# Perceiver layer on one core: the opening's loads, transposes and scalars issued in another order

## The reference

```python
x = x + cross(layernorm(x), ctx)   # K_hat = cos((ctx Wk + bk) Wr + br); softmax((xn Wq + bq) K_hat^T) (ctx Wv + bv)
x = x + attn(layernorm(x))         # the 8 most similar earlier tokens of h, softmax over them, message from h
    # mix = sigmoid(log_mix); scale = softplus(log_scale) + 0.01
    # gelu((mix h + (1 - mix) message) * gain + bias) * scale
x = x + moe(layernorm(x))          # 8 experts, one per token by argmax: gelu(x W1 + b1) W2 + b2, times the top probability
```

## Time and profile before

| | us |
|---|---|
| median of 3 runs | 442.94 |
| lowest, highest | 440.27, 447.44 |
| profiled execution, whole | 446.33 |
| its span, first to last instruction | 444.2 |
| TensorE busy in the span | 411.5 (93%) |
| VectorE, ScalarE, GpSimd busy | 248.5, 255.9, 237.7 |

### The profile page before, as it was taken

How to read it: one execution, slowest core, us unless ns; L and a number is a source line. 1 busy time by engine, 2 the same in 40 slices (tenths; PEclk the granted TensorE clock), 3 DMA queues, 4 the chain that set the end, 5 groups by cost and what they waited for, 6 DMA issues and landing times.

```text
span 444.2 us, 10438 instructions
## 1 busy us (share of the span) xinstructions
PE 411.5 (93%) x3121; PEld 281.9 (63%) x3121; DVE 248.5 (56%) x808; ACT 255.9 (58%) x582; POOL 237.7 (54%) x458
## 2 busy tenths in 40 slices
PE   7977999999999999999898878889999999999991
PEld 7423445454455544545344667679999999998991
DVE  2637478878988888788788655543222222222210
ACT  1474777888888988888678745253333232424240
POOL 1760567767788788888667765451222232222210
PEclk9987999999999999999999998999999999999997
DMA  9897899896986987789999624765685656465100
GB/s 174 188 251 214 216 273 273 202 214 174 278 186 150 240 202 212 185 206 260 190 296 310 220 79 132 234 173 206 239 304 187 200 180 217 165 192 198 57 0 2
DMA packets 119450, 87.46 MB, mean 197 GB/s; under 512 B 78622, under 2 KB 109088, under 8 KB 119268
## 3 DMA queue, kind: packets, MB, share of 16 engines
q1 hardware_dynamic: 111460, 75.96, 62.7%
q0 software_dynamic: 3744, 9.46, 7.0%
q10 hardware_dynamic: 4192, 1.38, 1.7%
HBM read 79.15 MB, written 8.53 MB: 197 GB/s over the span
## 4 chain that ended last, share of the span: by engine, by line
PE 71%; SPq 15%; issue 4%; DMA 4%; DVE 2%; ACT 1%; another core or an unknown queue 1%; POOL 0%; DVEq 0%; ACTq 0%; POOLq 0%
PE pK L1513 19%; PE pT L1500 17%; SPq L575 10%; PE pK L1475 8%; PE pT L1475 7%; PE b L1420 3%; SPq L570 3%; PE b L1659 3%; PE b L1554 3%; PE b L1619 2%; PE b L1598 2%; DMA f_row<-rows_by_token,token_i 2%; DMA token_i<-tokens_by_expert 2%; SPq L563 1%; PE b L1648 1%
## 5 line engine op out<-in xcount | busy, mean ns | idle before, releaser
L1272 ACT ACTIVATE XF<-pT,b_now 128x128 f32<-128x128 f32 x184 | 52.7, 370 | 97.1 <-PE pT L1500 91.8
L1513 PE MATMUL pK<-W,XF 128*128 x368 | 86.6, 387 | 5.9 <-issue 4.1
L1500 PE MATMUL pT<-XF,stage 128*128 128x128 f32 x736 | 87.0, 275 | 0.3 <-issue 0.3
L1500 PEld LDWEIGHTS pT<-XF,stage 128*128 128x128 f32 x736 | 85.9, 192 | 2.1 <-issue 1.1
L1513 PEld LDWEIGHTS pK<-W,XF 128*128 128x128 f32 x368 | 68.8, 193 | 15.5 <-issue 6.9
L409 POOL DMA_INDIRECT f_row<-rows_by_token,token_i x23 | 23.8, 1035 | 83.3 <-DMA out_dram<-XF,token_i 70.3
L1475 PE MATMUL pK<-stage,Wkr 128*128 128x512 f32 x128 | 63.0, 618 | 0.0
L1475 PE MATMUL pT<-stage,Wkr 128*128 128x512 f32 x128 | 61.8, 606 | 1.1 <-DVE stage L726 1.1
L1247 ACT ACTIVATE stage<-stage 128x512 f32<-128x512 f32 x64 | 40.7, 637 | 12.8 <-DVE stage L787 12.6
L787 DVE TENSOR_TENSOR stage<-stage 128x512 f32<-128x512 f32 x64 | 46.2, 722 | 0.7
L726 DVE STREAM_TRANSPOSE stage<-XF 128x1024 f32<-128x1024 f32 x32 | 39.5, 1234 | 12.4 <-DMA XF<-in_ctx_dram 11.3
(11 more groups left out here) (196 smaller groups left out, 666.1 us busy)
## 6 DMA issues: line engine op xcount, KB each, us to landing
stage<-in_L_ffn_W_dram SPq DMA_DIRECT2D x23, 1024.0 KB, 5.4
stage<-in_ctx_dram SPq DMA_DIRECT2D x32, 512.0 KB, 5.4
XF<-in_ctx_dram SPq DMA_DIRECT2D x248, 64.0 KB
W<-in_L_ffn_W_dram SPq DMA_DIRECT2D x8, 1024.0 KB
rows_by_token<-rows_out SPq DMA_DIRECT2D x16, 256.5 KB
ctx_last<-in_ctx_dram SPq DMA_DIRECT2D x64, 32.0 KB, 4.5
X<-in_x_dram SPq DMA_DIRECT2D x1, 1536.0 KB, 7.8
tokens_by_expert<-no_token POOLq DMA_DIRECT2D x2, 576.0 KB, 4.2
```

The lines of the kernel that those rows point to most:

```text
L1272: ins = act.activation(f_hT[b][:, n * P:(n + 1) * P], pT[i][:, (n % 4) * P:(n % 4 + 1) * P], ACT.Gelu, bias=b1_now[:, b, n:n + 1])
L1500: mm = pe.matmul(pT[i][:, (n % 4) * P:(n % 4 + 1) * P], W1[q][:, c, n * P:(n + 1) * P], f_inT[:, q % 2, c * P:(c + 1) * P], start=c == 0, ...
L1513: mm = pe.matmul(p_out, f_hT[q % 2][:, n * P:(n + 1) * P], W2[:, bass.ds(e, 1), n, :].rearrange("p o d -> p (o d)"), start=n == 0, stop=n ...
```

## The change

SyncE issues (1, 0)'s first part only; ScalarE issues its second. The rows of group 0 come next, then (1, 1), then (2, 0), and only then bv, Wv, the rows of group 1 and the small weights. GpSimd loads the two logs at the start. ScalarE issues Wq, bq, Wqk first, computes the scalars ahead of its half of `Wkr`, issues the second part of (1, 0), and loads the Sin table after that; `turn(0, 1)`, `turn(0, 3)` and `sine(0, 0, 2)` move forward by a place each, and in step 1 the Exp table is loaded right behind `turn(1, 0)`. VectorE turns (0, 1) before its first `whole` and (1, 0) after the third unit, and does its scalars in the prologue. TensorE's `ctx_project(1, 0, 1)` stands behind scores(0) and xn_T(1), as in later steps. The mask of own tokens is built with the other masks. At g = 15 `load_tokens(0)` stands ahead of `next_group(15)`.

```diff
--- before.py
+++ after.py
@@ -326,6 +326,8 @@
             keep(ident[:], [[-1, P]], 0, 1, ALU.not_equal, 1.0)
             made_at["ident"] = n[0]
             made(pool.memset(minus_half[:], -0.5))
+            for k, name in enumerate(("log_mix", "log_scale")):
+                pool.dma_start(logs[:, k:k + 1], a["L0_attn_" + name].partition_broadcast(P)).then_inc(S["logs_ld"], 16)
             rstd_x(0)
             normal_x(0)
@@ -363,13 +365,13 @@
                     for j in range(BG):
                         keep(t[j * T:(j + 1) * T, :], [[-1, T]], 0, 1, ALU.is_gt, fill)
                 made(pool.memset(unpicked[:], UNPICKED))
-                made_at["masks"] = n[0]
-
-            def own_parts():
-
                 made(pool.memset(own_part[:], 0.0))
                 for j in range(BG):
                     keep(own_part[j * T:(j + 1) * T, :], [[-1, T]], 0, 1, ALU.not_equal, 1.0)
+                made_at["masks"] = n[0]
+
+            def own_parts():
+
                 pool.wait_ge(S["scal_dve"], 3)
                 made(pool.tensor_scalar(own_part[:], own_part[:], sc[:, 2:3], None, ALU.mult))
@@ -582,20 +584,19 @@
                 sp.dma_start(last_rows[:, k * P:(k + 1) * P].rearrange("b (a n) -> b a n", n=T),
                              in_blocks(c_in[:, CF, :], k)).then_inc(S["last_ld"], 16)
             sp.wait_ge(S["ctxT_r"], 1)
-            for j in range(2):
-                load_by_feature(1, 0, j)
+            load_by_feature(1, 0, 0)
+            load_ctx(0, 0)
+            load_last(0, 0)
             sp.wait_ge(S["ctxT_r"], 2)
             for j in range(2):
                 load_by_feature(1, 1, j)
-            load_ctx(0, 0)
-            load_last(0, 0)
+            sp.wait_ge(S["ctxT_r"], 3)
+            for j in range(2):
+                load_by_feature(2, 0, j)
             sp.dma_start(bv[:], a["L0_xattn_bv"].partition_broadcast(P)).then_inc(S["bv_ld"], 16)
             sp.dma_start(Wv[:], rows(a["L0_xattn_Wv"])).then_inc(S["w_ld"], 16)
             load_ctx(1, 1)
             load_last(1, 1)
-            sp.wait_ge(S["ctxT_r"], 3)
-            for j in range(2):
-                load_by_feature(2, 0, j)
             sp.dma_start(gain[:], a["L0_attn_gain"].partition_broadcast(P)).then_inc(S["w_ld"], 16)
             sp.dma_start(gbias[:], a["L0_attn_bias"].partition_broadcast(P)).then_inc(S["w_ld"], 16)
             sp.dma_start(Wroute[:], rows(a["L0_ffn_Wr"])).then_inc(S["w_ld"], 16)
@@ -653,6 +654,8 @@
                     sp.wait_ge(S["ctxT_r"], 2 * g + 1)
                     for j in range(2):
                         load_by_feature(g + 1, 0, j)
+                if g == NG - 1:
+                    load_tokens(0)
                 next_group(g, g % 2)
                 if g == 2:
                     sp.wait_ge(S["consts"], made_at["routing"])
@@ -660,8 +663,6 @@
                         sp.dma_start(by_token[TOK + i:TOK + i + 1, :], rows_out[0:1, 0, :]).then_inc(rows_st[i], 16)
                 if g >= 3 and g % 2:
                     load_w2(g // 2 - 1)
-                if g == NG - 1:
-                    load_tokens(0)
                 if g % 2 and g >= 7:
                     keep((g - 7) // 2)
                 if g == NG - 2:
@@ -1025,17 +1026,18 @@
                 v.wait_ge(S["xn_r"], g)
                 moments(g, st1, mv1, "st1_r", "mv1_r")
+            ctx_turned(0, 1)
             whole(0, 0)
             fraction(0, 0)
-            ctx_turned(0, 1)
             next_stats(1)
             whole(0, 1)
             fraction(0, 1)
             next_moments(1)
             last_copy()
-            ctx_turned(1, 0)
+            scalars()
             whole(0, 2)
             fraction(0, 2)
+            ctx_turned(1, 0)
             last_turned()
             whole(0, 3)
             fraction(0, 3)
@@ -1100,8 +1102,6 @@
                 residual(s - 1)
                 if s >= 4:
                     logits_copy(s - 4)
-                if s == 1:
-                    scalars()
                 if s == 13:
                     plan_experts(0)
                 if s == 14:
@@ -1215,22 +1215,23 @@
             for q in range(P // T):
                 act.dma_start(*quarter_by_feature(0, 1, 1, q)).then_inc(by_feature_ld[1], 16)
             act.wait_ge(S["consts"], made_at["ident"])
-            act.activation(sumA[:], ident[:, 0:1], ACT.Sin)
+            act.dma_start(Wq[:], rows(a["L0_xattn_Wq"])).then_inc(S["wq_ld"], 16)
+            act.dma_start(bq[:], col(a["L0_xattn_bq"]), allow_slow_non_contiguous=True).then_inc(S["wq_ld"], 16)
+            act.dma_start(Wqk[0:H, :], a["L0_attn_W_q"]).then_inc(S["wqk_ld"], 16)
+            act.dma_start(Wqk[H:2 * H, :], a["L0_attn_W_k"]).then_inc(S["wqk_ld"], 16)
+            act.wait_ge(S["logs_ld"], 2 * 16)
+            act.activation(sc[:, 0:1], logs[:, 0:1], ACT.Exp, scale=-1.0).then_inc(S["scal_act"], 1)
+            act.activation(sc[:, 5:6], logs[:, 1:2], ACT.Abs).then_inc(S["scal_act"], 1)
+            act.wait_ge(S["scal_act"], 2)
+            act.activation(sc[:, 6:7], sc[:, 5:6], ACT.Exp, scale=-1.0).then_inc(S["scal_act"], 1)
+            act.wait_ge(S["scal_act"], 3)
+            act.activation(sc[:, 7:8], sc[:, 6:7], ACT.Ln, bias=1.0).then_inc(S["scal_act"], 1)
             act.wait_ge(S["wkr_mm"], 2)
             act.mul(Wkr[:, 1, :], pT[1][:, 0:D], INV_2PI).then_inc(S["wkr_half"], 1)
-            act.dma_start(bq[:], col(a["L0_xattn_bq"]), allow_slow_non_contiguous=True).then_inc(S["wq_ld"], 16)
-            act.dma_start(Wq[:], rows(a["L0_xattn_Wq"])).then_inc(S["wq_ld"], 16)
-            act.dma_start(Wqk[0:H, :], a["L0_attn_W_q"]).then_inc(S["wqk_ld"], 16)
-            act.dma_start(Wqk[H:2 * H, :], a["L0_attn_W_k"]).then_inc(S["wqk_ld"], 16)
-
-            def scalars():
-                act.wait_ge(S["logs_ld"], 2 * 16)
-                act.activation(sc[:, 0:1], logs[:, 0:1], ACT.Exp, scale=-1.0).then_inc(S["scal_act"], 1)
-                act.activation(sc[:, 5:6], logs[:, 1:2], ACT.Abs).then_inc(S["scal_act"], 1)
-                act.wait_ge(S["scal_act"], 2)
-                act.activation(sc[:, 6:7], sc[:, 5:6], ACT.Exp, scale=-1.0).then_inc(S["scal_act"], 1)
-                act.wait_ge(S["scal_act"], 3)
-                act.activation(sc[:, 7:8], sc[:, 6:7], ACT.Ln, bias=1.0).then_inc(S["scal_act"], 1)
+            act.wait_ge(S["ctxT_r"], 1)
+            for q in range(P // T):
+                act.dma_start(*quarter_by_feature(1, 0, 1, q)).then_inc(by_feature_ld[0], 16)
+            load_table(ACT.Sin, 0)
             def turn(g, u):
@@ -1317,31 +1318,29 @@
             act.wait_ge(S["bkr_cp"], 1)
             turn(0, 0)
+            turn(0, 1)
             act.dma_start(X[:, 2:4, :], x_v[:, 2:4, :]).then_inc(S["xnext_ld"], 16)
-            turn(0, 1)
             xnT_copy(0)
             sine(0, 0, 0)
-            act.dma_start(logs[:, 0:1], a["L0_attn_log_mix"].partition_broadcast(P)).then_inc(S["logs_ld"], 16)
-            act.dma_start(logs[:, 1:2], a["L0_attn_log_scale"].partition_broadcast(P)).then_inc(S["logs_ld"], 16)
             sine(0, 0, 1)
             turn(0, 2)
+            turn(0, 3)
             queries(0)
+            sine(0, 0, 2)
             act.wait_ge(S["last_fr"], 4)
             act.activation(khat_last[:], last_frac, ACT.Sin, scale=TWO_PI).then_inc(S["khat_last_r"], 1)
-            turn(0, 3)
-            sine(0, 0, 2)
             sine(0, 0, 3)
             for s in range(1, NG):
                 if s >= 3:
                     second_exp(s - 3)
                 turn(s, 0)
+                if s == 1:
+                    load_table(ACT.Exp, 1)
                 xnT_copy(s)
                 first_exp(s - 1)
                 if s >= 7 and s % 2:
                     router_exp(s // 2 - 3)
-                if s == 1:
-                    scalars()
                 if s >= 4:
                     gelu_y(s - 4)
                 probsT_copy(s - 1)
@@ -1680,15 +1679,12 @@
             for s in range(1, NG):
                 ctx_project(s, 0, 0)
-                if s == 1:
-                    ctx_project(s, 0, 1)
                 scores(s - 1)
                 if s >= 7 and s % 2:
                     pe.wait_ge(S["logits_r"], s - 4)
                     rank(s // 2 - 3)
                 xn_T(s)
-                if s >= 2:
-                    ctx_project(s, 0, 1)
+                ctx_project(s, 0, 1)
                 probs_T(s - 1)
                 if s >= 2:
                     h_T(s - 2)
```

## The result

The changed kernel takes 446.31 us (median of 20 runs, 443.77 to 450.07), the kernel before 443.10 beside it (20 runs). The ratio is 1.0087, 95% interval [1.0058, 1.0117]: slower by 3.9 us or 0.9%, clear of noise but within the 2% that the chances were given for. The forecast was 436.4 and its range 432.0 to 441.0; the result lies above the range, and its sign is the other one.

A forecast was written before the change was run, and what follows sets the result against it. TensorE was taken as the bound (71% of the span), with 9.8 us to draw on in two early steps. Terms -5.5 - 2.1 + 0.6 + 0.5 = -6.5 us gave 436.4 against the 442.94 median; eight in ten between 432.0 and 441.0.

The forecast's parts named there:

- the mechanism of step 1 up to (2, 0): Step 1: SyncE issues (2, 0) earlier, so it is turned at 30.1 instead of 35.5, 5.4 us earlier.
- step 1 at -5.5: Step 1's gain: step 2 starts at 36.1, not 41.62; -5.5 us, bounds -3.5 and -6.5.
- After that, before took 41.62 - 35.5 = 6.1 us to step 2: Step 1 behind (2, 0)'s turn: the old 6.1 us, less 1.0 plus 0.9, puts step 2 at 36.1.
- the clock, -2.1: Step 2: full clock expected instead of mean 0.87, as no idle stretch over 1 us precedes; -2.1 us, bounds 0 and -2.3.
- -2.1 + 0.6: Step 2: -2.1 us from the full clock, +0.6 from VectorE's wait for (3, 0) behind the load of all of X.
- The rival that had the clock fall again (0.18): Opening and step 2: idle ahead of the first projection lowers the clock, step 2's 2.1 us stay; 438 to 440, chance 0.18.
- the opening: Prologue: first projection at 12.0, not 9.97, 2.0 us late; scores(0) at 24.9 against 24.56, between 23.7 and 26.6.
- it costs nothing until 9.6: Opening: loading the two logs through GpSimd costs nothing if they are there by 9.6, when the Exp table is.
- the merge, +0.5: Step 15, load_tokens(0) ahead of next_group(15): SyncE stands 3.2 us, W1(0) may come late; +0.5 us, bounds -1.1 and +2.1.
- the gain is 1.1 at most: Step 15: an earlier token load can save at most TensorE's 1.09 us wait for gather(0)'s rows.
- A microsecond won before 57.93 should come off the end unless a transfer can't follow: Whole kernel: time won before step 3 at 57.93 shortens the total, unless a transfer can't follow.
- a rival (0.10): Steps 1 and 2: transfers can't follow, the wait moves to (3, 0) at +3, merge +2.1; 440.4, chance 0.10.

The follow-up runs named there:

- e3: The changed kernel with bv, Wv, gain, gbias, Wroute and b1 issued between (1, 1) and (2, 0); 1.0018 of the kernel before.
- e4: The changed kernel with load_tokens(0) back behind next_group(15) and the weights issued ahead of (2, 0); 0.9973 of the kernel before, 0.9964 when repeated.
- g1: e4 with the rest of X in three loads and ScalarE doing Exp load, `Wkr` scaling, weight issues, then scalars; 0.9973 of the kernel before, 0.9932 when repeated.
- e8: e4 with the rest of X in three loads, the first W2 at g = 6, and `Wkr` scaling ahead of the scalar chain; 0.9873 of the kernel before.
- e1: The changed kernel with load_tokens(0) moved back behind next_group(15); 1.0018 of the kernel before.
- e2: The kernel before with only load_tokens(0) moved ahead of next_group(15); 1.0081 of the kernel before.

## Why the prediction was wrong

**Right: the mechanism of step 1 up to (2, 0).** The forecast had (2, 0) turned by 30.1 in place of 35.5; the trace has the transpose from 30.36 to 31.6, so 4.0 of the 5.4 us came. No wait over 1 us there; the clock of 28.60 to 32.00 back at 1.00. TensorE's 2.34 and 2.35 us of idle were gone.

**Wrong: step 1 at -5.5.** The step that failed is "After that, before took 41.62 - 35.5 = 6.1 us to step 2". That stretch was forecast at 36.1 - 30.1 = 6.0 us and took 40.59 - 31.6 = 9.0. The step followed TensorE, ScalarE and VectorE behind (2, 0) and never asked which loads value_project(0) waits for. `w_ld` was the next wait in line: in the kernel before it was met at 36.1, 3 us ahead of use, and the same edit put a megabyte in front of it. The text's "the rows and weights behind it by 31.8" was off too: SyncE was through with them at 35.0, since (2, 0)'s quarters were issued until 27.84 and not 25.9. value_project(0) went at the same 39.3 as before, and 4.5 of the 5.5 us stayed out: 1.5 had been lost by (2, 0), 3.0 behind it. e3 and e4 show it by moving these loads ahead of (2, 0); worth 0.4 to 0.7%.

**Wrong: the clock, -2.1.** "With no idle stretch over 1 us in front I expect the full clock" had a false premise; the idle stretch was the 3.44 us just told. Step 2 took 15.88 us, 0.4 less than before and not 1.5 (-2.1 + 0.6); e4, without that stretch, has the forecast's 14.8. The rival that had the clock fall again (0.18) was right at both of its places, the opening (5.37 us for 3.70) and step 2 (0.89), and too small in the sum.

**Wrong in size: the opening.** The half was scaled at 12.41, forecast at 11.5. ScalarE's issues of Wq and bq took 1.00 and 0.68 us where they had taken 0.49 and 0.39, so its list ended at 9.16 and not 8.3. GpSimd's logs landed at 9.0, not 7.8, and just in time. But "it costs nothing until 9.6" looked at the logs' own user alone: the two loads go with the half-empty DMA engines of 4 to 6 us and with context quarters that land 1.4 us late (g1 above). In the changed kernel that delay hides behind ScalarE's scaling; with the scaling early, in g1 and e8, it is the bound. With the low clock behind it, scores(0) came at 26.79, the late bound (26.6) and not 24.9. ScalarE's timeline, after:

```profile
6.44 1.00 ACTq L1218 DMA_DIRECT2D Wq<-in_L_xattn_Wq_dram  x1
7.47 0.68 ACTq L1219 DMA_DIRECT2D bq<-in_L_xattn_bq_dram  x1
...
9.16 1.28 ACT L1223 ACT_TABLE_LOAD   x1 [9.16 <-issue]
...
11.01 1.28 ACT L1228 ACT_TABLE_LOAD   x1
...
12.30 0.20 ACT L1228 ACTIVATE sc<-sc 128x1 f32<-128x1 f32 x1
12.41 0.37 ACT L1230 ACTIVATE Wkr<-pT 128x256 f32<-128x256 f32 x1
```

Two loads, as counted, and no pause behind either: the activation follows the load of 11.01 by 1.29 us. The Trainium skill (ScalarE: Activation LUTs, What ACT_TABLE_LOAD costs) adds a drain of some 1.38 us to each; the trace doesn't show one.

**Wrong in place and size: the merge, +0.5.** The step that failed is "the gain is 1.1 at most". SyncE's hole was foreseen (3.2 us, measured 4.4), and so were the empty engines; the bill was sent to W1(0), when the first to want a landing in that heap was gather(0) itself, at +3.9 us of wait and about 2 us at the low clock behind it. At 0.7 to 0.8% (e1, e2) this one move, in place of +0.5 us, costs 3 us or more.

**Missing: the lead is not kept.** "A microsecond won before 57.93 should come off the end unless a transfer can't follow" left its last clause to a rival (0.10) that looked at steps 1 and 2 alone. It was the nearest to right of all: e4 had 3.8 us in hand at step 3 in its trace and gained 1.2 by its ratio; with W2's bytes out, 4.3 and 4.1. That a lead is lost, and that fewer bytes keep it, the ratios show as far as their intervals go; at which place, no run settles.

In sum: the change has a part worth about -1.2 us (e4), a weight order that takes 2 to 3 us away and a token load that takes 2 to 3.6; the measured 3.9 us lie within what the three add up to, 2.8 to 5.4. Place by place, in the two traces, the forecast had -7.0 at step 3 and the result -1.5; the lead was 1.7 us before step 15, and there the forecast had +0.5 and the result +5.8. These two gaps, 5.5 and 5.3 us, are about the 10.4 us between forecast and result.

## What to carry to other kernels

When a wait is taken away, list every semaphore that the next few instructions wait for, with the landing of each before the change: the second to last one is the new bound, above all where the same edit puts bytes in front of it. A load that waits for a late value must not stand ahead of bulk loads on one queue, since these come back as a heap on top of the next small transfer that is on the path. A load moved to another engine can delay the transfers of its neighbours, so look at the DMA share around it and not at its own user alone. And where the DMA engines are busy for most of a loop (0.84 to 0.96 here between 60 and 150 us), don't count time won ahead of it as kept; a test run without most bytes of one tensor tells whether they are what takes it.
